# Audio tower, second layer: the loop written out with its branch hint ahead of the last chunk, GpSimd's slot work spread over chunks, wo's sums ahead of the gated product on VectorE

## The reference

```python
h = tok(x); h = h + attn0(layernorm(h)); h = h + ffn0(layernorm(h))     # first layer
# second layer, attention: b = 64 clips, H = 16 heads, D = 64, M = 64 features
q = heads(x @ wq.T); k = heads(x @ wk.T); v = heads(x @ wv.T)
phi(t) = exp(t @ omega.T - 0.5 * sum(t * t)) / sqrt(M)
out = causal_linear_attention(phi(q), phi(k), v)     # cumulative sums over time
h = h + out @ wo.T + bo
# second layer, feed-forward, F = 1024
x4 = layernorm(h)                                    # the input of the block
h5 = layernorm(x4) * ln_g + ln_b
y = silu(h5 @ w1 + fc1_bias)
h = h + x4 + 0.5 * (y @ w2 + fc2_bias)
```

## Time and profile before

| | |
|---|---|
| median of three runs | 4857.81 us (4853.75 to 4859.07) |
| the profiled execution's own time | 4853.85 us |
| its span in the trace | 4852.1 us |
| granted TensorE clock, mean over the span | 0.983 |
| busy: PE / PEld / DVE / ACT / POOL | 93% / 80% / 68% / 51% / 38% |
| first layer and constants, second layer's start and end in the span | about 0 to 1850, 1850 and 4852 us |

### The profile page before, as it was taken

The page is one execution under the profiler, slowest core; times in us unless marked ns, Lnnn a source line. Parts: engine busy times, 40 slices in busy tenths (PEclk is TensorE's granted clock), DMA queues, the critical chain, the costliest instruction groups (busy, mean ns, idle before and its releaser), DMA issues.

```text
span 4852.1 us, 118621 instructions
## 1 busy us (share of the span) xinstructions
PE 4530.7 (93%) x42264; PEld 3883.6 (80%) x42264; DVE 3322.7 (68%) x7101; ACT 2486.4 (51%) x5312; POOL 1855.5 (38%) x2018
## 2 busy tenths in 40 slices
PE   3999999999999985999999999999999999999997
PEld 2777777777777764888888888888888888888886
DVE  4888888888888863566666666666666666666565
ACT  1555555555555543455555555555555545555453
POOL 1444444444444432334334334334334334334333
PEclk9999999999999997999999999999999999999998
DMA  2000000000000001000000000000000000000000
GB/s 81 19 23 23 20 23 23 23 19 23 23 23 19 23 14 41 5 8 11 11 8 11 11 8 11 11 8 11 11 8 11 11 8 11 11 8 11 11 5 10
DMA packets 64927, 79.21 MB, mean 16 GB/s; under 512 B 8758, under 2 KB 51126, under 8 KB 64438
## 3 DMA queue, kind: packets, MB, share of 16 engines
q1 hardware_dynamic: 64566, 74.07, 5.3%
HBM read 49.40 MB, written 24.64 MB: 15 GB/s over the span
## 4 chain that ended last, share of the span: by engine, by line
PE 47%; POOL 5%; issue 4%; DVE 3%; ACT 2%; ACTq 0%; POOLq 0%; DMA 0%; DVEq 0%; SPq 0%
PE bA L912 10%; PE bA L913 8%; PE bA L914 8%; PE bS L1198 3%; PE bO L1221 3%; PE bA L1285 2%; PE bB L912 2%; PE bB L1185 2%; PE bB L1184 2%; PE bB L913 2%; PE bB L914 2%; PE bA L1286 1%; POOL res L1602 1%; POOL res L1600 1%; POOL sqs_lo L1583 1%
## 5 line engine op out<-in xcount | busy, mean ns | idle before, releaser
L1583 POOL TENSOR_TENSOR sqs_lo<-sq,sqs_hi 128x768 fp32r<-128x768 f32 x256 | 477.2, 1864 | 917.5 <-ACT sqs_hi L1338 909.8
L1429 DVE TENSOR_TENSOR qk_lo<-bA,qk_hi 128x384 fp32r<-128x384 f32 x512 | 283.4, 554 | 625.2 <-ACT qk_hi L1338 625.0
L1357 ACT ACTIVATE phi<-bB 128x768 f32<-128x768 f32 x256 | 207.8, 812 | 700.5 <-PE bB L1185 700.5
L1575 POOL TENSOR_TENSOR yT_lo<-tanh_y,yT_hi 128x384 fp32r<-128x384 f32 x256 | 258.9, 1011 | 566.7 <-ACT yT_hi L1338 566.7
L1338 ACT ACTIVATE qk_hi<-bA 128x384 fp32r<-128x384 f32 x512 | 251.2, 491 | 212.7 <-PE bA L914 212.7
L1439 DVE TENSOR_TENSOR aT<-bS,mask 128x1024 f32<-128x1024 f32 x256 | 311.0, 1215 | 1.2 <-PE bS L1203 1.2
L1347 ACT ACTIVATE sq<-bA 128x384 f32<-128x384 f32 x512 | 250.2, 489 | 64.1 <-DVE qk_lo L1429 64.1
L507 PE MATMUL bank<-down_sb,hqT 128*128 128x256 f32 x1128 | 279.9, 390 | 1.0 <-ACT hqT L588 1.0
L604 ACT ACTIVATE kblk<-gu,kb_masked,rowmask 128x128 f32<-128x128 f32 x752 | 270.6, 461 | 6.2 <-PE gu L531 6.2
L463 PE MATMUL gu<-gate_sb,xqT 128*128 128x352 f32 x752 | 265.3, 476 | 1.1 <-ACT xqT L588 1.1
L507 PEld LDWEIGHTS bank<-down_sb,hqT 128*128 128x128 f32 x1128 | 207.8, 191 | 72.6 <-issue 33.0
(11 more groups left out here) (230 smaller groups left out, 14547.5 us busy)
## 6 DMA issues: line engine op xcount, KB each, us to landing
xT<-in_x SPq DMA_DIRECT2D x94, 256.0 KB, 2.6
h_scratch<-h SPq DMA_DIRECT2D x188, 64.0 KB, 1.9
hx<-h_scratch SPq DMA_DIRECT2D x32, 256.0 KB, 2.7
out<-res SPq DMA_DIRECT2D x32, 256.0 KB, 2.1
hx<-h_scratch SPq DMA_DIRECT2D x64, 64.0 KB, 2.4
out<-res SPq DMA_DIRECT2D x64, 60.0 KB, 1.9
q<-in_fc_q SPq DMA_DIRECT2D x2, 1024.0 KB, 6.3
wq_sb<-in_wq SPq DMA_DIRECT2D x1, 1024.0 KB, 4.9
```

The lines of the kernel that those rows point to most:

```text
L1429: dve.tensor_tensor(dst, src, hi.bitcast(fp32), ALU.subtract).then_inc(S[done], 1)
L1583: pool.tensor_tensor(sqs[1][:], sq[:], sqs[0][:].bitcast(fp32), ALU.subtract).then_inc(S["sq_lo"], 1)
```

## The change

Four things change, all in `layer1`.

1. `slots` writes the loop out by hand instead of `nc.Fori(..., hint_back_edge=True)`. The branch hint moves, on every engine, from the first instruction of an iteration to the place ahead of its last chunk. The number of TensorE's instructions in an iteration stays the same.
2. GpSimd's slot work gets a function of its own, `slot_work`, called at the start of a step, ahead of that chunk's `sqs_lo`. The pieces that stood at the end of chunks 4 and 5 now stand at the start of 5 and 6, with nothing between. What stood at the end of chunk 6 is taken apart: `rs5` and then `res = h3 + x4` at the start of 7; `res + fc2b` at the start of chunk 2 of the next slot; `h3 = hx + bo` at the start of chunk 1 of the slot that uses it. `x4 * ln_g`, `x4 + ln_b` go from the end of 7 to the start of 0, again with nothing between.
3. On VectorE, at place 0 of a step, a v copy or wo's sums now come ahead of the gated product `fc1_y`; at places 1 and 2 the order stays.
4. VectorE's last normalisation of a slot waits for the first of the two additions to res alone.

```diff
             for s in range(-1, 3):
                 slot(s, s % 2)
-            with nc.Fori(3, last, 2, engines=(eng.engine,), hint_back_edge=True) as s:
+            engines = (eng.engine,)
+            name = f"layer1_slots_{nc.next_id()}"
+            index = nc.alloc_registers(f"{name}_i", engines=engines)
+            nc.regs_mov(index, 3)
+            nc.br(f"{name}_loop", engines=engines)
+            with nc.body(f"{name}_loop", valid_engines=engines):
+                s = nc.snap(index, min_val=3, max_val=last - 1)
                 slot(s, 1)
-                slot(s + 1, 0)
+                for c in range(CH):
+                    if c == CH - 1:
+                        jump = eng.mark_branch_hint_location()
+                    step(s + 1, c, 0)
+                nc.regs_alu(index, index, 2, op=ALU.add)
+                eng.br_lt(index, last, on_true=f"{name}_loop", on_false=f"{name}_end").branch_hint(jump)
+            nc.switch_bb(f"{name}_end")
...
                 def place(s, c, n, par):
+                    if n == 0:
+                        run_place(dict(v=v_pair, wo=wo_pair), s, c, n, par)
                     run_place(dict(fc1=fc1_y), s, c, n, par, 1)
-                    run_place(dict(v=v_pair, wo=wo_pair, fc1=fc1, fc2=fc2_pair, xn=xn_transpose, h5=h5_transpose),
-                              s, c, n, par)
+                    run_place(dict(fc1=fc1, fc2=fc2_pair, xn=xn_transpose, h5=h5_transpose), s, c, n, par)
...
                     if c == 7 and has_slot(s - 1):
                         wait(dve, "rs5", s, 2)
-                        wait(dve, "res_step", s, 2)
+                        dve.wait_ge(S["res_step"], (s - 1) * 2 + 1)
                         normalize(s - 1, 2, x4, x4, "h5_ready")
...
+                def slot_work(s, c, par):
+
+                    if c == 0 and has_slot(s - 2):
+                        wait(pool, "h5_ready", s - 1, QT)
+                        pool.tensor_tensor(x4[:], x4[:], bc(lng_bc), ALU.mult).then_inc(S["h5_gb"], 1)
+                        pool.wait_ge(S["h5_gb"], (s - 2) * 2 + 1)
+                        pool.tensor_tensor(x4[:], x4[:], bc(lnb_bc), ALU.add).then_inc(S["h5_gb"], 1)
+                    if c == 1 and has_slot(s):
+                        wait(pool, "h2_loaded", s + 1, 48)
+                        if not isinstance(s, int) or s >= 2:
+                            pool.wait_ge(S["res_step"], (s - 2) * 2 + 1)
+                        pool.tensor_tensor(h3[par][:], hx[:], bc(bo_bc), ALU.add).then_inc(S["h3_start"], 1)
+                    if c == 2 and has_slot(s - 2):
+                        r = res[par]
+                        pool.wait_ge(S["res_step"], (s - 2) * 2 + 1)
+                        pool.tensor_tensor(r[:], r[:], bc(fc2b_bc), ALU.add).then_inc(S["res_step"], 1)
...
+                    if c == 7 and has_slot(s - 1):
+                        wait(pool, "stat5", s, 2 * QT)
+                        wait(pool, "h5_ready", s - 1, QT)
+                        rsqrt(s - 1, 2, "rs5")
+                        r = res[1 - par]
+                        if not isinstance(s, int) or s - 3 >= 0:
+                            pool.wait_ge(S[f"out_stored{1 - par}"], (s - 3) * 24 + (48 - 24 * (1 - par)))
+                        pool.tensor_tensor(r[:], h3[1 - par][:], x4[:], ALU.add).then_inc(S["res_step"], 1)
+
                 def step(s, c, par):
                     g, b = s * CH + c, c % 2
+                    slot_work(s, c, par)
                     run_place(dict(fc1=fc1_lo), s, c, 0, par, 2)
...
-                    if c == 6 and has_slot(s - 1):
-
-                        wait(pool, "x4_ready", s, QT)
-                        r = res[1 - par]
-                        if not isinstance(s, int) or s - 3 >= 0:
-                            pool.wait_ge(S[f"out_stored{1 - par}"], (s - 3) * 24 + (48 - 24 * (1 - par)))
-                        pool.tensor_tensor(r[:], h3[1 - par][:], x4[:], ALU.add).then_inc(S["res_step"], 1)
-                        pool.wait_ge(S["res_step"], (s - 1) * 2 + 1)
-                        pool.tensor_tensor(r[:], r[:], bc(fc2b_bc), ALU.add).then_inc(S["res_step"], 1)
-                        wait(pool, "stat5", s, 2 * QT)
-                        wait(pool, "h5_ready", s - 1, QT)
-                        rsqrt(s - 1, 2, "rs5")
-                    if c == 6 and has_slot(s + 1):
-                        wait(pool, "h2_loaded", s + 2, 48)
-                        wait(pool, "res_step", s, 2)
-                        pool.tensor_tensor(h3[1 - par][:], hx[:], bc(bo_bc), ALU.add).then_inc(S["h3_start"], 1)
```

More of the change, by code:

```diff
@@ L1576, in fc1_lo @@
                                        ALU.subtract).then_inc(S["y_lo"], 1)
+                def slot_work(s, c, par):
[13 more added lines that the diff above has]
+                        pool.tensor_tensor(r[:], r[:], bc(fc2b_bc), ALU.add).then_inc(S["res_step"], 1)
+                    if c == 5 and has_slot(s + 1):
+                        wait(pool, "stat3", s + 2, 2 * QT)
+                        wait(pool, "xn_ready", s + 1, QT)
+                        rsqrt(s + 1, 0, "rs3")
+                    if c == 6 and has_slot(s - 1):
+                        wait(pool, "stat4", s, 2 * QT)
+                        wait(pool, "x4_ready", s - 1, QT)
+                        rsqrt(s - 1, 1, "rs4")
+                    if c == 7 and has_slot(s - 1):
[6 more added lines that the diff above has]
+                        pool.tensor_tensor(r[:], h3[1 - par][:], x4[:], ALU.add).then_inc(S["res_step"], 1)
                 def step(s, c, par):
                     g, b = s * CH + c, c % 2
+                    slot_work(s, c, par)
                     run_place(dict(fc1=fc1_lo), s, c, 0, par, 2)
```

## The result

The changed kernel takes 4829.16 us (4828.41 to 4830.64, four runs) against 4856.42 us for the kernel before: ratio 0.9946, 95% interval 0.9930 to 0.9962, so 27 us less, where 15 were forecast. Of the range that the prediction gave its main case (4829 to 4852) that is the lower edge. The profiled execution took 4828.62 us with a span of 4826.3, 25.8 under the span of before.

A forecast was written before the change was run, and what follows sets the result against it. TensorE's own work was taken to bound the kernel, so only its stops could be won. Terms -25 - 7.6 - 16 + 29.4 + 4.5 = -14.7 us gave 4843 us against the median, with a range of 4808 to 4860.

The forecast's parts named there:

- main case: Whole kernel: the summed terms hold, 4843 us, own range 4829 to 4852; chance 0.55.
- The sign: Whole kernel: faster, given 0.67, against 0.25 for the same and 0.08 for slower.
- the rival that the hint works in full: Loop's back edge: each TensorE branch falls to 0.22 us, 10 us less than the sum, 4833; chance 0.12.
- GpSimd at a slot's end: Chunk 7: TensorE's wait for `sqs_lo` goes, margin 0.7 us; 1.49 us at each of 17 ends without branch, -25 us.
- The branch behind it: Back edge, 12 places: branch ends together with `sqs_lo`, then takes 1.1 us; -7.6 us, bounds -1.7 to -18.
- the lower bound of 1.7: Back edges: gain of 1.7 us if TensorE's branches stay as long as they are.
- wo's sums at chunk 5: Chunk 5: TensorE no longer waits for the sums on VectorE, 0.54 us a slot, 30 slots, -16 us.
- Chunk 3: Gated product, now after wo's sums, is held by POOL's `sqs_lo`; fc2 0.98 us later, 30 slots, +29 us.
- The first rival: Chunk 3: the gated product is not held up, +29.4 becomes about -3, time 4811 us; chance 0.17.
- Chunk 6: The product, behind the v copy, overlaps `sqs_lo` and lengthens it; 0.15 us a slot, 30 slots, +4.5 us.
- The slower rival: TensorE's new stops at chunk 3 each bring 1.2 GHz periods, 1.7 us each, 4882 us; chance 0.08.

The follow-up runs named there:

- run 11: The kernel before with TensorE's code 64 instructions further on and nothing else, hint at the loop's head: 4851.06 us, ratio 0.9996.
- run 7: The changed kernel with 64 more instructions on TensorE ahead of the second layer, so its loop code lies further on: 4822.60 us, ratio 0.9933.
- run 8: The changed kernel with no branch hint on any engine: 4863.31 us, ratio 1.0015.
- run 5: The changed kernel with GpSimd's yT_lo of f = 1 moved ahead of its `sqs_lo` at chunk 3: 4793.47 us, ratio 0.9870.
- run 3: The changed kernel with VectorE's order of before at place 0, gated product ahead of v copy and wo's sums: 4817.98 us, ratio 0.9927.
- run 4: The changed kernel with the gated product back ahead of wo's sums at chunk 3 alone: 4798.92 us, ratio 0.9888.
- run 2: The kernel before with only GpSimd's slot work spread and VectorE's shorter wait; loop and VectorE's order of before: 4823.39 us, ratio 0.9938.
- run 1: The kernel before with only the loop written out and the hint ahead of the last chunk on every engine: 4851.31 us, ratio 0.9991.
- run 12: The changed kernel with TensorE's code 64 instructions further on and the gated product ahead of wo's sums again at chunk 5 alone: 4829.05 us, ratio 0.9943.

## Why the prediction was right, and its size 12 us short

The sign, the likeliest case and the mechanisms but that of the branch held; the size was 27 us instead of 15. The number by itself could not have told: 4829 is nearer to the price of the rival that the hint works in full (4833) than to 4843. It is the branches of the trace, 1.6 us in the mean, that speak against that rival. In the loop, 11.6 us more were won than forecast: 4.9 at the 14 slot ends, 3.7 at chunk 5, 2.8 at chunk 6, 1.1 at chunk 3 and 2.0 elsewhere, less 2.9 at the back edges, where the gain was smaller than said.

**GpSimd at a slot's end.** Right: the wait is gone with the margin forecast (0.8 us, 0.7 said). The term was mis-sized: 1.49 us an end instead of 1.78 in the median (with 1.0 us of half clock, which one such end of before had, the 14 make 25.8). I took the gap of the records for the cost of a stop. A matmul of 0.34 us in the records is followed by the next 0.17 us after its start, so a gap begins 0.17 us later than the next matmul would have; and the first matmul behind it holds up the next one for 0.28 us (3013.69 to 3013.97), against 0.20 with no stop (2922.17 to 2922.37). That makes 1.49 + 0.17 + 0.08 = 1.74 of the 1.77. The same holds at chunk 5: 0.54 us of gap, 0.68 of time. Over all 17 ends and 30 slots the two are 9 of the 12 us.

**The branch behind it.** That branch and `sqs_lo` end together was right, as run 11 shows. The step "it goes elsewhere. I take 1.1 us per branch ... from that alone" failed: the load of hx was moved and the branches stayed at 1.6 us in the mean. I had asked the right question, what sets the fetch's moment, and named the answer, TensorE's arrival in the last block of code, but priced the term by another. Runs 7 and 11 bear it out: 64 instructions more ahead of the loop move the fetch from about 1 to 6 us ahead, with the hint at either place. In run 8 a fetch starts ahead of the branch at that same place with no hint at all. The rival that the hint works in full fell. The back edges still gave 4.7 us, above the lower bound of 1.7.

The Trainium skill (Runtime: NRT & Kernel Launch, Instruction fetch mechanics) says that prefetch is purely sequential, and that a taken branch out of the window forces a fetch. Run 8 fits that sentence, with its fetch behind the branch's start and 3.5 us a branch; with a hint the measurement decides against it, since the target's fetch comes up to 6 us ahead.

**wo's sums at chunk 5.** Right, and 3.7 us larger in the loop by the cost of a stop. That the product of this chunk would be held up just as at chunk 3 was overlooked; nothing waited for it, so the sum did not suffer.

**Chunk 3.** Right in each step: the product held to 0.42 us behind `sqs_lo` (0.41 forecast), fc2 later by it, +24.4 us in the loop against +25.5. Run 5 shows the cause by taking POOL's instruction away, runs 3 and 4 the price. The first rival, that the product is not held, fell: it would have given 4811. The Trainium skill (SBUF — State Buffer, SBUF: two separate sides) says that the port pair shared by VectorE and GpSimd is an exclusive lock for the length of an instruction; the traces agree: the product of f = 1 took 1.72 to 1.80 us in all 26 slots of the loop, and 0.55 in all 26 of run 5.

**Chunk 6.** Mis-sized: +0.04 us a slot for the 0.15 said. In even slots the product begins 0.36 us ahead of `sqs_lo` and overlaps it by 0.19 only, and `sqs_lo` takes 1.88; in odd slots it overlaps by 0.12, and `sqs_lo` takes 1.82 as before.

**The clock.** The slower rival did not come in the changed kernel: no half-clock stretch behind 26 new stops, two in the loop where before had six. Run 7 shows that it was a true danger: the same stops, 9 stretches, 14 us. Half clock less often at the back edge is also most of what the table has under "the others" and a part of the 4.7 us. Other runs with such stops had three or four at slot ends (runs 2, 4, 5 and 11), none (run 3) or six (run 1), so as far as these runs tell that is scatter between executions. Run 8, whose stops at the back edge are twice as long, had ten there.

## What to carry to other kernels

A stop of TensorE costs more than the gap in the records: here 0.28 us more between matmuls of 384 columns, and 0.14 at chunk 5, ahead of matmuls of 256. Before an instruction of VectorE with two inputs in SBUF is put behind another one, look what GpSimd does at its new moment; if a long instruction of it stands there and TensorE soon needs what the held one makes (chunk 3, not chunk 5), change GpSimd's order, provided that its long instruction is not needed soon. For a loop whose body is fetched as it runs, look for the fetch ahead of the back edge: if it starts late, keep the hint where it is and move the code, or write the loop out.

## What was not expected of the hardware

- The time of TensorE's taken branch is set by where the code lies: 1.5 us in the median with the branch as compiled, 0.36 us with 64 instructions more ahead of the loop, 3.5 us with no hint.
- The same stop of 1.7 us at the same chunk was followed by 3.4 us at 1.2 GHz in no iteration of the changed kernel, in 1 of 13 of run 12, in 2 of 13 of run 8 and in 9 of 13 of run 7. What decides between them stays open.
